# Laying a block diagonal by SBUF-to-SBUF transfers from SyncE, and one mean made earlier

## Chip, cores and metric

One core of a Trainium2 chip runs the kernel. The metric is the device time of one execution in microseconds.

## The reference

The kernel computes a small feed-forward block with a conditioned input. x is 32 x 32 x 256 (batch, channel, feature), 1024 token rows in all.

```python
w = weights[conditions]                       # 32 of 200 matrices, each 32 x 32
xc = jnp.einsum('bct,bcd->bdt', x, w)         # channel mix, per batch item
def _rmsnorm(x, g): return g * (x * rsqrt(mean(x * x) + EPS))
def _act_quant(x):                            # 8-bit steps per row
    scale = 127.0 / clip(max(abs(x)), 0.0001)
    return clip(round(x * scale), -128, 127) / scale
def _ternary_quant(w):
    s = mean(abs(w))
    return round(tanh(w / (s + EPS))) * arctanh(s)
def _linear_bit(x, w, g): return einsum('bsd,od->bso', _act_quant(_rmsnorm(x, g)), _ternary_quant(w))
h = silu(_linear_bit(xc, w1, g1)) * _linear_bit(xc, w2, g2)     # hidden width 1024
out = x + _linear_bit(h, w3, g3)
```

## The kernel before

The 1024 token rows are eight tiles of 128 rows, worked on as four pairs in the first half and tile by tile in the second. Every engine has its own program, written out by hand, and runs it in order; semaphores join them. There is no planner.

The first half prepares the operands. A tile holds four batch items of 32 channels, so the channel mix of a tile is one matmul with a 128 x 128 block diagonal, `cw_diag[:, tile, :]`, of four gathered 32 x 32 matrices. GpSimd zeroes `cw_diag` (L214, `diag_zero`), then gathers the rows of the condition weights by eight indirect transfers, one for a tile (L218), into `cw_rows`; `cw_in[p]` reaches 32 when both tiles of pair p have landed. On VectorE `diagonal(p)` (L441 to L446) copies the 32 x 32 blocks of pair p from `cw_rows` onto the diagonal with four copies, one for each group of 32 partitions and both tiles at once. TensorE's `condition(p)` (L645 to L654) waits for these four copies and for the x of the pair and makes `xc_ps`. ScalarE's `x_squares(p)` (L348) takes the sums of squares, VectorE's `x_gains(p)` (L471) multiplies by g1 and g2, `x_peak_of(p)` takes the largest magnitude, `x_scales(p)` the scale; `x_round(p)` is split between GpSimd and ScalarE (all VectorE for pair 3). TensorE's `x_turn(p)` transposes and VectorE's `x_keep(p)` writes the operand.

Weights: each of W1, W2, W3 is loaded in two halves of 512 KB (L159). The sums of magnitudes are made by ScalarE for first halves and by VectorE for second halves of W1 and W2 (`abs_sum_half`, L434), by ScalarE for both halves of W3. TensorE's `total(m)` adds over partitions, VectorE's `mean(m)` (L448 to L455) gives the mean and its inverse, ScalarE's `tanh(m)` (L344) uses it, `round_w(m)` rounds (W1 on VectorE, W2 and W3 on GpSimd), `w_turn` transposes, `keep_w` writes.

Orders around the change:

- SyncE (L164 to L191): cond; W1 half 0, W1 half 1, W2 half 0; W2 half 1 behind W1 half 0; x pair 0 behind W1 half 1; g1 and g2 behind W2 half 0; x pair 1 behind W2 half 1; W3 half 0 behind x pair 0; W3 half 1 behind x pair 1; x pair 2 behind W3 half 0; x pair 3 behind W3 half 1; g3 behind x pair 2; then the eight stores.
- VectorE (L512 to L540): two half sums, mean(0), diagonal(0), mean(1), diagonal(1), round_w(0), x_gains(0), x_peak_of(0), diagonal(2), x_gains(1), diagonal(3), x_scales(0), x_peak_of(1), mean(2), keep_w(0, 1), x_gains(2), and so on.
- TensorE (L705 to L718): total(0), total(1), condition(0), condition(1), the two w_turn of W1, condition(2), total(2), condition(3), x_turn(0), the two w_turn of W2, x_turn(1).
- ScalarE (L374 to L392): two half sums, tanh(0), x_squares(0), tanh(1), x_squares(1), the two half sums of W3, x_squares(2), x_round(0), keep_w_a(0), tanh(2), x_round(1), x_squares(3), keep_w_a(1), x_round(2), the logarithm.
- GpSimd (L281 to L293): x_roots(0), x_roots(1), round_w(1), x_round(0), x_roots(2), arctanh_start, x_round(1), x_roots(3), x_round(2), arctanh_rest, arctanh_end, round_w(2). arctanh_end releases `xdeq_ready`, for which the first gate (`silu(0)`, L399) waits.

The second half runs over eight tiles: two up projections, gate, product, RMS norm with g3 on GpSimd (L325), rounding, transposes, down projection, residual and store.

Of the kernel before, what the change touches and what calls it, by code (L numbers as in the profile page):

```python
# [14 lines left out]
BATCH, CHAN, FEAT = 32, 32, 256  # L15
HID = 1024
TOKENS = BATCH * CHAN
TILES = TOKENS // P
PAIRS = TILES // 2
PER_TILE = P // CHAN  # L20
# [13 lines left out]
def adaln_ffn(nc, x, cond, cond_w, w1, g1, w2, g2, w3, g3, out):  # L34
    ctx = ExitStack()
    with ctx:
        def sb(name, shape, dt=FP32):
            return ctx.enter_context(nc.sbuf_tensor(name, shape, dt))

        def sem(name):  # L40
            return ctx.enter_context(nc.semaphore(name))
# [22 lines left out]
        cw_rows = sb("cw_rows", [P, TILES, CHAN])  # L64
        cw_diag = sb("cw_diag", [P, TILES, P])
# [55 lines left out]
        cw_in = [sem(f"cw_in{p}") for p in range(PAIRS)]  # L121
# [3 lines left out]
        xr_a, wq_a, neg_made = sem("xr_a"), sem("wq_a"), sem("neg_made")  # L125
        rounder_made, roots_made, diag_zero = sem("rounder_made"), sem("roots_made"), sem("diag_zero")
        cond_cast, chan_made, idx_summed, idx_ready = sem("cond_cast"), sem("chan_made"), sem("idx_summed"), sem("idx_ready")
        diag_ready = [sem(f"diag{p}_ready") for p in range(PAIRS)]

        abs_a, abs_v, tot_ready, mean_ready, inv_ready = sem("abs_a"), sem("abs_v"), sem("tot_ready"), sem("mean_ready"), sem("inv_ready")  # L130
        tanh_done, w_rounded, wt_ready, wq_ready = sem("tanh_done"), [sem(f"w{m + 1}_rounded") for m in range(3)], sem("wt_ready"), sem("wq_ready")
# [23 lines left out]
        @block.sync  # L155
        def _(sp):
            def load_w(m, h):
                n = w_sb[m].shape[1] // 2
                sp.dma_start(w_sb[m][:, h * n:(h + 1) * n, :], w_rows[m][:, h * n:(h + 1) * n, :]).then_inc(w_in[m][h], 16)  # L159

            def load_x(p):
                sp.dma_start(x_sb[:, 2 * p:2 * p + 2, :], x_rows[:, 2 * p:2 * p + 2, :]).then_inc(x_in[p], 16)

            sp.dma_start(cond_i[:], cond.rearrange("(t b) -> b t", b=PER_TILE), allow_slow_non_contiguous=True).then_inc(cond_in, 16)  # L164
            load_w(0, 0)
            load_w(0, 1)
            load_w(1, 0)

            sp.wait_ge(w_in[0][0], 16)
            load_w(1, 1)  # L170
            sp.wait_ge(w_in[0][1], 16)
            load_x(0)
            sp.wait_ge(w_in[1][0], 16)
            for k, g in enumerate((g1, g2)):
                sp.dma_start(g12[:, k, :], g.partition_broadcast(P)).then_inc(g12_in, 16)
            sp.wait_ge(w_in[1][1], 16)
            load_x(1)
            sp.wait_ge(x_in[0], 16)
            load_w(2, 0)
            sp.wait_ge(x_in[1], 16)  # L180
            load_w(2, 1)
            sp.wait_ge(w_in[2][0], 16)
            load_x(2)
            sp.wait_ge(w_in[2][1], 16)
            load_x(3)
            sp.wait_ge(x_in[2], 16)
            sp.dma_start(g3_all[:], g3.partition_broadcast(P)).then_inc(g3_in, 16)
            for t in range(TILES):
                sp.wait_ge(out_ready, t + 1)
                sp.dma_start(out_rows[:, t, :], x_sb[:, t, :]).then_inc(stored, 16)  # L190
            sp.wait_ge(stored, 16 * TILES)  # L191
# [233 lines left out]
        def _(dve):  # L425
# [8 lines left out]
            def abs_sum_half(m):  # L434

                n = w_sb[m].shape[1] // 2
                dve.wait_ge(w_in[m][1], 16)
                dve.tensor_reduce(abs_sum[:, 2 * m + 1:2 * m + 2], w_sb[m][:, n:, :], AX.XY, ALU.add,  # L438
                                  apply_absolute_value=True).then_inc(abs_v, 1)

            def diagonal(p):  # L441

                dve.wait_ge(cw_in[p], 32)
                for b in range(PER_TILE):
                    s = slice(b * CHAN, (b + 1) * CHAN)
                    dve.tensor_copy(cw_diag[s, 2 * p:2 * p + 2, s], cw_rows[s, 2 * p:2 * p + 2, :]).then_inc(diag_ready[p], 1)  # L446

            def mean(m):  # L448

                dve.wait_ge(tot_ready, m + 1)  # L450
                dve.tensor_scalar(mean_abs[:, m:m + 1], tot_ps[m], 1.0 / n_weights, None, ALU.mult).then_inc(mean_ready, 1)
                dve.wait_ge(mean_ready, m + 1)
                dve.tensor_scalar(eps_mean[:, m:m + 1], mean_abs[:, m:m + 1], EPS, None, ALU.add).then_inc(mean_step, 1)
                dve.wait_ge(mean_step, m + 1)
                dve.reciprocal(inv_mean[:, m:m + 1], eps_mean[:, m:m + 1]).then_inc(inv_ready, 1)  # L455

            def round_w(m):
                dve.wait_ge(tanh_done, m + 1)
                dve.tensor_scalar(w_sb[m][:], w_sb[m][:], ROUNDER, None, ALU.add).then_inc(w_rounded[m], 1)
# [11 lines left out]
            def x_gains(p):  # L471

                dve.wait_ge(xss_ready, 2 * (p + 1))
                if p == 0:
                    dve.wait_ge(g12_in, 32)
                for k in range(2):
                    dve.tensor_tensor(xg[:, p, k], xc_ps[p % 2],  # L477
                                      g12[:, k, :].unsqueeze(1).to_broadcast([P, 2, FEAT]), ALU.mult).then_inc(xg_ready, 1)

            def x_peak_of(p):  # L480
                dve.wait_ge(xg_ready, 2 * (p + 1))
                dve.tensor_reduce(x_peak[:, p], xg[:, p], AX.X, ALU.max,  # L482
                                  apply_absolute_value=True).then_inc(xpeak_ready, 1)

            def x_scales(p):

                dve.wait_ge(xpeak_ready, p + 1)
                dve.wait_ge(xroot_ready, p + 1)
                dve.scalar_tensor_tensor(x_step[:, p], x_peak[:, p], 1.0 / QMAX,
                                         x_root[:, p, 0, :].unsqueeze(1).to_broadcast([P, 2, 2]), ALU.mult, ALU.max  # L490
                                         ).then_inc(xstep_ready, 1)
                dve.wait_ge(xstep_ready, p + 1)
                dve.reciprocal(x_scale[:, p], x_step[:, p]).then_inc(xscale_ready, 1)
                dve.tensor_tensor(x_deq0[:, p], x_step[:, p],
                                  x_root[:, p, 1, :].unsqueeze(1).to_broadcast([P, 2, 2]), ALU.mult).then_inc(xdeq0_ready, 1)
# [14 lines left out]
                                  ALU.add).then_inc(xq_ready, 1)  # L510

            abs_sum_half(0)  # L512
            abs_sum_half(1)
            mean(0)
            dve.wait_ge(diag_zero, 1)
            diagonal(0)
            mean(1)
            diagonal(1)
            round_w(0)
            x_gains(0)  # L520
            x_peak_of(0)
            diagonal(2)
            x_gains(1)
            diagonal(3)
            x_scales(0)
            x_peak_of(1)
            mean(2)
# [113 lines left out]
        def _(pe):  # L641
# [2 lines left out]
            pe.matmul(idx_ps, group32[:], cond_f[:], start=True, stop=True).then_inc(idx_summed, 1)  # L644
            def condition(p):  # L645

                pe.wait_ge(diag_ready[p], PER_TILE)
                pe.wait_ge(x_in[p], 16)
                if p >= 2:
                    pe.wait_ge(xg_ready, 2 * (p - 1))  # L650
                for i in range(2):
                    last = pe.matmul(xc_ps[p % 2][:, i, :], cw_diag[:, 2 * p + i, :], x_sb[:, 2 * p + i, :],  # L652
                                     start=True, stop=True)
                last.then_inc(xc_ready, 1)  # L654
# [51 lines left out]
            total(0)  # L706
            total(1)
            condition(0)
            condition(1)
            w_turn(0, 0)  # L710
            w_turn(0, 1)
            condition(2)
            total(2)
            condition(3)
# [98 lines left out]
```

## Time and profile before

| | us |
|---|---|
| median of 3 runs | 78.03 |
| lowest and highest run | 77.39, 78.25 |
| span of the profiled execution, first to last instruction | 76.6 |
| busy in the span: VectorE, GpSimd, TensorE, ScalarE | 58.1, 55.4, 48.0, 47.7 |

The page has no time of the profiled execution beside its span, so the span is set beside the runs. VectorE is the busiest engine over the whole span, but busy shares are averages over two halves with different limits. The first half ends where the first gate starts, at 34.47 us. "Idle before" in a timeline is the time in which the engine did nothing, with what ended it.

### The profile page before, as it was taken

The page shows a single profiled execution, that of the slowest core. Times are in us where ns is not written, and L with a number is a line of the kernel's source. Part 1 is how long each engine was busy: PE and PEld are TensorE (multiplying, and loading weights), DVE is VectorE, ACT ScalarE, POOL GpSimd, SP SyncE. Part 2 cuts the span into 40 slices and gives each one's busy share as a digit, 9 for nine tenths or more (in the row PEclk, how much of TensorE's full clock was granted, in tenths as well). Part 3 has the DMA queues.
Part 4 walks back from the last instruction along what each step waited for, and adds up shares of the span by engine and source line. Part 5 has one row for each costly group of instructions (what it writes and reads, how often), then busy time and mean ns, then how long its engine had stood idle before and what let it go on. Part 6 is the DMA issues. An engine that isn't in the chain of part 4 may idle for free.

```text
span 76.6 us, 1068 instructions
## 1 busy us (share of the span) xinstructions
PE 48.0 (63%) x298; PEld 31.3 (41%) x302; DVE 58.1 (76%) x117; ACT 47.7 (62%) x70; POOL 55.4 (72%) x97
## 2 busy tenths in 40 slices
PE   0200509995829803999897298977888471079960
PEld 0200408774526702355461155544545250078730
DVE  0203278989999999967699989979797979996340
ACT  5014508599909995995859959896979783410000
POOL 6788777264938977989689898999999999810100
PEclk9999999999975895556999999999999999855589
DMA  0599989963710000000000000010202020010222
GB/s 0 119 385 346 327 237 278 330 210 115 253 71 0 0 0 4 0 9 4 0 0 0 0 0 4 17 52 9 68 0 68 0 68 0 23 45 0 68 68 68
DMA packets 5369, 6.22 MB, mean 81 GB/s; under 512 B 500, under 2 KB 4980, under 8 KB 5364
## 3 DMA queue, kind: packets, MB, share of 16 engines
q1 hardware_dynamic: 5108, 6.03, 24.6%
q0 software_dynamic: 256, 0.13, 0.8%
q8 instruction: 2, 0.03, 0.2%
q14 instruction: 3, 0.02, 0.1%
HBM read 5.11 MB, written 1.05 MB: 80 GB/s over the span
## 4 chain that ended last, share of the span: by engine, by line
DVE 24%; issue 22%; POOL 22%; DMA 12%; PE 11%; ACT 4%; SPq 0%; POOLq 0%; DVEq 0%
DMA w_sb<-in_L_ffn_w 12%; POOL hg L325 11%; PE y_ps L769 6%; DVE xg L477 6%; DVE cw_diag L446 5%; DVE x_peak L482 5%; PE a_ps L652 3%; PE t_ps L758 2%; POOL h_deq L302 2%; DVE hid L551 2%; ACT hr L413 2%; DVE abs_sum L438 2%; POOL h_root L316 2%; POOL h_base L311 2%; POOL h_base L309 1%
## 5 line engine op out<-in xcount | busy, mean ns | idle before, releaser
L325 POOL TENSOR_TENSOR hg<-hid,g_all 128x1024 f32<-128x1024 f32 x7 | 16.5, 2358 | 0.8 <-DVE hid L551 0.8
L413 ACT ACTIVATE hr<-hg,rounder,h_scale 128x1024 f32<-128x1024 f32 x7 | 8.7, 1241 | 5.5 <-DVE h_scale L574 5.5
L769 PE MATMUL y_ps<-w_t,hq_t 128*128 128x256 bf16 x64 | 10.3, 319 | 2.1 <-DVE hq_t L581 2.0
L560 DVE TENSOR_REDUCE h_peak<-hg 128x1 f32<-128x1024 f32 x8 | 9.7, 1217 | 1.7 <-POOL hg L325 1.6
L551 DVE SCALAR_TENSOR_TENSOR hid<-v_ps,x_deq,gate 128x1024 f32<-128x1024 f32 x8 | 10.2, 1271 | 0.9 <-PE v_ps L725 0.6
L725 PE MATMUL v_ps<-w_t,xq_t 128*128 128x512 bf16 x30 | 8.9, 415 | 3.0 <-DVE hid L551 2.9
L399 ACT ACTIVATE gate<-a_ps,x_deq 128x1024 f32<-128x1024 f32 x8 | 8.8, 1100 | 2.2 <-PE a_ps L725 2.1
L725 PE MATMUL a_ps<-w_t,xq_t 128*128 128x512 bf16 x30 | 8.7, 407 | 1.8 <-issue 1.3
L218 POOL DMA_INDIRECT cw_rows<-in_L_cond_weights,row_idx x8 | 7.9, 982 | 2.4 <-issue 2.1
L769 PEld LDWEIGHTS y_ps<-w_t,hq_t 128*128 128x128 bf16 x64 | 6.9, 115 | 5.6 <-DVE hq_t L581 4.1
L652 PE MATMUL a_ps<-x_sb,cw_diag 128*128 128x256 f32 x16 | 7.0, 597 | 2.5 <-DVE cw_diag L446 2.5
L758 PE MATMUL t_ps<-ident,hr 128*128 128x128 f16 x64 | 5.8, 243 | 4.2 <-ACT hr L413 4.2
L406 ACT ACTIVATE h_sq_junk<-hid 128x1024 bf16<-128x1024 f32 x8 | 8.4, 1046 | 0.0
L341 ACT ACTIVATE abs_values<-w_sb 128x1024 bf16<-128x1024 f32 x4 | 4.2, 1061 | 5.2 <-DMA w_sb<-in_L_ffn_w 5.2
L346 ACT ACTIVATE w_sb<-w_sb,inv_mean 128x2048 f32<-128x2048 f32 x3 | 6.0, 1999 | 2.2 <-DVE inv_mean L455 2.2
L667 PE MATMUL y_ps<-abs_sum,ones 128*128 128x1 f32 x12 | 2.5, 317 | 7.6 <-DVE abs_sum L438 7.2
L758 PEld LDWEIGHTS t_ps<-ident,hr 128*128 128x128 f16 x64 | 4.8, 110 | 6.0 <-ACT hr L413 4.7
L438 DVE TENSOR_REDUCE abs_sum<-w_sb 128x1 f32<-128x1024 f32 x2 | 2.4, 1220 | 5.4 <-DMA w_sb<-in_L_ffn_w 5.4
L302 POOL TENSOR_SCALAR h_deq<-h_step,h_root,atanh 128x1 f32<-128x1 f32 x8 | 3.6, 455 | 3.5 <-DVE x_sb L588 3.5
L316 POOL TENSOR_TENSOR h_root<-h_base,roots 128x2 f32<-128x2 f32 x8 | 5.6, 702 | 0.7
L725 PEld LDWEIGHTS v_ps<-w_t,xq_t 128*128 128x128 bf16 x32 | 2.8, 104 | 7.8 <-DVE hid L551 5.0
L581 DVE TENSOR_SCALAR hq_t<-t_ps 128x1024 bf16<-128x1024 f16 x8 | 5.5, 683 | 0.6 <-PE t_ps L758 0.6
(76 smaller groups left out, 99.9 us busy)
## 6 DMA issues: line engine op xcount, KB each, us to landing
w_sb<-in_L_ffn_w SPq DMA_DIRECT2D x6, 512.0 KB, 4.5
x_sb<-in_x SPq DMA_DIRECT2D x4, 256.0 KB, 3.1
out<-x_sb SPq DMA_DIRECT2D x8, 128.0 KB, 1.7
g_all<-in_L_ffn_g SPq DMA_DIRECT2D x1, 512.0 KB, 4.3
g<-in_L_ffn_g SPq DMA_DIRECT2D x2, 128.0 KB
cw_rows<-in_L_cond_weights,row_idx POOLq DMA_INDIRECT x8, 4.3
cond_i<-in_itok_B SPq DMA_DIRECT2D x1, 0.1 KB
```

What stands on the lines that cost most here:

```text
L218: pool.indirect_dma_start(cw_rows[:, t, :], None, cond_rows, bass.IndirectOffsetOnAxis(ap=row_idx[:, t:t + 1].bitcast(UINT32), axis=0)).th ...
L316: pool.tensor_tensor(h_root[:, b], h_base[:, b], roots[:, :, 0], ALU.pow).then_inc(hroot_ready, 1)
L325: pool.tensor_tensor(hg[:, b], hid[:, b], g3_all[:], ALU.mult).then_inc(hg_ready, 1)
L399: act.activation(gate[:, t % 2], a_ps[:], ACT.Silu, scale=x_deq[:, 0, t // 2, t % 2:t % 2 + 1]).then_inc(gate_ready, 1)
L406: act.activation(h_sq_junk[:, t % 2], hid[:, t % 2], ACT.Square, accum_out=h_ss[:, t % 2:t % 2 + 1]).then_inc(hss_ready, 1)
L413: act.activation(hr[:, t % 2], hg[:, t % 2], ACT.Identity, scale=h_scale[:, t % 2:t % 2 + 1], bias=rounder[:]).then_inc(hr_ready, 1)
L551: dve.scalar_tensor_tensor(hid[:, t % 2], v_ps[:], x_deq[:, 1, t // 2, t % 2:t % 2 + 1], gate[:, t % 2], ALU.mult, ALU.mult).then_inc(hid_ ...
L560: dve.tensor_reduce(h_peak[:, b], hg[:, t % 2], AX.X, ALU.max, apply_absolute_value=True).then_inc(hpeak_ready, 1)
L652: last = pe.matmul(xc_ps[p % 2][:, i, :], cw_diag[:, 2 * p + i, :], x_sb[:, 2 * p + i, :], start=True, stop=True)
L725: last = pe.matmul(ps[:, n * HALF:(n + 1) * HALF], xq_t[:, which, c, t * P:(t + 1) * P], w_t[which][:, c, n * HALF:(n + 1) * HALF], start= ...
L758: last = pe.transpose(t_ps[t % 2][:, j * P:(j + 1) * P], low_half(hr[:, t % 2, j * P:(j + 1) * P]), ident[:])
L769: last = pe.matmul(y_ps[t % 2][:, 0:FEAT], hq_t[:, t % 2, j, :], w_t[2][:, j, :], start=(j == 0), stop=(j == KH - 1))
```

## The change

- The copies of `diagonal` leave VectorE. SyncE gets a `diagonal(i)` of its own, with i = 0, 1, 2 for pair 0, pair 1, and pairs 2 and 3 together. It waits for the gathers of these pairs and issues four transfers from `cw_rows` to `cw_diag`, one for each group of 32 partitions: 32 partitions by two tiles (four tiles for i = 2) by 128 bytes.
- They are placed in SyncE's order: diagonal(0) behind x pair 0 (with a wait for the zeroed tile), diagonal(1) behind x pair 1, diagonal(2) behind x pair 2.
- TensorE's `condition(p)` waits for the transfers (64 counts of `diag_in`) instead of the four copies; pairs 2 and 3 share one semaphore.
- VectorE's `mean(0)` moves ahead of `abs_sum_half(1)`, the sum of W2's second half.

```diff
-        diag_ready = [sem(f"diag{p}_ready") for p in range(PAIRS)]
+        diag_in = [sem(f"diag_in{i}") for i in range(3)]
@@ SyncE
+            def diagonal(i):
+
+                for p in ((0,), (1,), (2, 3))[i]:
+                    sp.wait_ge(cw_in[p], 32)
+                tiles = slice(2 * i, (2, 4, TILES)[i])
+                for b in range(PER_TILE):
+                    s = slice(b * CHAN, (b + 1) * CHAN)
+                    sp.dma_start(cw_diag[s, tiles, s], cw_rows[s, tiles, :]).then_inc(diag_in[i], 16)
+
@@
             load_w(1, 1)
             sp.wait_ge(w_in[0][1], 16)
             load_x(0)
+            sp.wait_ge(diag_zero, 1)
+            diagonal(0)
             sp.wait_ge(w_in[1][0], 16)
             for k, g in enumerate((g1, g2)):
                 sp.dma_start(g12[:, k, :], g.partition_broadcast(P)).then_inc(g12_in, 16)
             sp.wait_ge(w_in[1][1], 16)
             load_x(1)
+            diagonal(1)
             sp.wait_ge(x_in[0], 16)
             load_w(2, 0)
             sp.wait_ge(x_in[1], 16)
             load_w(2, 1)
             sp.wait_ge(w_in[2][0], 16)
             load_x(2)
+            diagonal(2)
             sp.wait_ge(w_in[2][1], 16)
             load_x(3)
@@ VectorE
-            def diagonal(p):
-
-                dve.wait_ge(cw_in[p], 32)
-                for b in range(PER_TILE):
-                    s = slice(b * CHAN, (b + 1) * CHAN)
-                    dve.tensor_copy(cw_diag[s, 2 * p:2 * p + 2, s], cw_rows[s, 2 * p:2 * p + 2, :]).then_inc(diag_ready[p], 1)
-
@@
             abs_sum_half(0)
+            mean(0)
             abs_sum_half(1)
-            mean(0)
-            dve.wait_ge(diag_zero, 1)
-            diagonal(0)
             mean(1)
-            diagonal(1)
             round_w(0)
             x_gains(0)
             x_peak_of(0)
-            diagonal(2)
             x_gains(1)
-            diagonal(3)
             x_scales(0)
@@ TensorE, condition(p)
-                pe.wait_ge(diag_ready[p], PER_TILE)
+                pe.wait_ge(diag_in[min(p, 2)], 16 * PER_TILE)
```

## Rows read from the trace of the kernel before

**Rows 1.** Stretches: us, busy of each engine (instructions), granted clock, DMA share, GB/s

```profile
34.50:64.00 29.50, 23.13 (x167) 12.76 (x168) 26.23 (x40) 24.00 (x30) 26.91 (x34) 0.98 0.06 19
```

**Rows 2.** Chain of waits from 8 to 35 us: start, us, what

```profile
12.65 2.09 PE a_ps L652 x4
14.76 0.85 ACT x_sq_junk L351 x4
...
20.24 1.59 DVE cw_diag L446
...
30.54 0.94 POOL xr L243 x2
...
34.47 1.12 ACT gate L399
```

**Rows 3.** Timeline of SyncE's queue: start, us, line, what, idle before

```profile
6.91 0.37 SPq L162 DMA_DIRECT2D x_sb<-in_x  x1
8.46 0.83 SPq L175 DMA_DIRECT2D g<-in_L_ffn_g  x2
10.10 0.38 SPq L162 DMA_DIRECT2D x_sb<-in_x  x1
10.91 2.35 SPq L159 DMA_DIRECT2D w_sb<-in_L_ffn_w  x2
15.05 2.64 SPq L162 DMA_DIRECT2D x_sb<-in_x  x2
```

**Rows 4.** The page's list of issues: KB each, median us from issue to landing

```profile
out<-x_sb SPq DMA_DIRECT2D x8, 128.0 KB, 1.7
```

**Rows 5.** Line L218, all eight gathers: ns min/median/max, first and last start, landing

```profile
L218 POOL DMA_INDIRECT cw_rows<-in_L_cond_weights,row_idx x8: 944/944/1237, 3.8 to 12.9; - x8
...
DMA to landing us min/median/max: 3.6/4.3/4.9
```

**Rows 6.** Line L218 in the window of gather 1 alone

```profile
L218 POOL DMA_INDIRECT cw_rows<-in_L_cond_weights,row_idx x1: 955/955/955, 5.4 to 5.4; - x1
...
DMA to landing us min/median/max: 4.9/4.9/4.9
```

**Rows 7.** Timeline of TensorE, 8 to 20 us

```profile
8.28 0.98 PE L667 MATMUL y_ps<-abs_sum,ones 128*128 128x1 f32 x4 [5.03 <-DVE abs_sum L438]
...
16.22 1.91 PE L702 MATMUL t_ps<-ident,w_sb 128*128 128x128 f16 x16
18.97 1.13 PE L652 MATMUL a_ps<-x_sb,cw_diag 128*128 128x256 f32 x4 [0.84 <-DVE cw_diag L446]
```

**Rows 8.** Timeline of VectorE, 10 to 29 us

```profile
10.10 1.22 DVE L438 TENSOR_REDUCE abs_sum<-w_sb 128x1 f32<-128x1024 f32 x1 [1.97 <-DMA w_sb<-in_L_ffn_w]
...
20.15 2.33 DVE L446 COPY cw_diag<-cw_rows 32x64 f32<-32x64 f32 x4
...
23.98 0.15 DVE L451 TENSOR_SCALAR mean_abs<-y_ps 128x1 f32<-128x1 f32 x1
...
28.87 1.28 DVE L477 TENSOR_TENSOR xg<-a_ps,g 128x512 f32<-128x512 f32 x2
```

**Rows 9.** The tile of the gathered rows: the copies

```profile
L446 DVE COPY cw_diag<-cw_rows x16: 163/186/1671, 11.7 to 22.3; 32x64 f32<-32x64 f32 x16
```

**Rows 10.** Line L159, the six loads of the weights

```profile
DMA to landing us min/median/max: 4.1/4.5/6.2
```

**Rows 11.** Line L162, the four loads of x

```profile
DMA to landing us min/median/max: 2.7/3.1/4.0
```

**Rows 12.** Timeline of ScalarE, 20 to 28 us

```profile
20.17 0.39 ACT L351 ACTIVATE x_sq_junk<-a_ps 128x256 bf16<-128x256 f32 x1
...
22.92 1.09 ACT L358 ACTIVATE xr<-xg,rounder,x_scale 128x256 f32<-128x256 f32 x2 [1.90 <-DVE x_scale L493]
...
27.79 0.36 ACT L351 ACTIVATE x_sq_junk<-a_ps 128x256 bf16<-128x256 f32 x1
```

**Rows 13.** Timeline of GpSimd at 20 us

```profile
19.88 1.91 POOL L237 TENSOR_SCALAR w_sb<-w_sb 128x2048 f32<-128x2048 f32 x1
```

## Prediction

> **What bounds the kernel now.** I read the table of stretches first. From 34.5 to 64.0 us GpSimd is busy 26.91 of 29.50 us [rows 1]: a steady loop over the eight token tiles, in which nothing that the change touches is issued. So the change can only shift the moment at which that loop starts, and I take any shift of it one for one to the end. The span is 76.6 us; the runs around it are 78.03 us in the median, so 1.4 us lie outside the span, and I leave those as they are.
>
> The chain of waits says what sets that start [rows 2]. It enters the first matmul of `condition(0)` at 12.65, goes over ScalarE's squares and then stays almost wholly on VectorE until 30.5, where GpSimd's last `x_round` and the arctanh steps lead to the first gate at 34.47. The copies of `diagonal` lie on that chain: sixteen, in the median 186 ns [rows 9], so a group of four takes about 0.9 us with its gaps, but the group of `diagonal(3)` takes 2.33 us [rows 8], since its first copy, the longest of all (1671 ns), covers 1.59 us of the chain [rows 2, 9]. Read alone, this says that VectorE would win some 3 us in the stretch behind 18 us. ScalarE's timeline says how much room there is beside it: it idles only 1.90 us ahead of `x_round(0)` at 22.92, and then works without a gap to the squares of pair 3 at 27.79 [rows 12], whose end (28.6) comes 0.26 us ahead of `x_gains(3)` at 28.87 [rows 8]. So the second limit is 0.26 us away, and it begins with what releases ScalarE at about 21 us: the squares of pair 2, hence `condition(2)` on TensorE, which starts at 18.97 [rows 7].
>
> SyncE's own timeline is the view that decides [rows 3]. It is one in-order queue, and before the change its waits only touch transfers of their own kind. It shows each load's issue; the landings are in the answers on the lines [rows 4, 5, 10, 11].
>
> **The change part by part.**
>
> *1. mean(0) moved ahead of the sum of W2's half.* VectorE idles 1.97 us before that sum at 10.10 [rows 8]. The total of W1 can be made at once behind the first half sum: its four short matmuls run from 8.28 to 9.26 [rows 7], so mean(0) runs at 9.3 to 9.9, inside that idle time, and the tanh of W1 starts near 9.9 instead of 11.8. Its price is nothing (if the cover were gone, it would cost its own 0.5 us). Its gain is nothing either: what follows the tanh on ScalarE is the squares of pair 0, which wait for TensorE at 14.76 [rows 2], and mean(1) still waits for the half sum that starts at 10.10.
>
> *2. Sixteen copies leave VectorE.* That frees two groups of 0.9 us ahead of `round_w(0)`, which comes forward by about 1 us into nothing that waits (TensorE turns W1 behind condition(1)), and 0.9 + 2.33 us around x_gains(1). After it, `x_scales(0)` can follow `x_gains(1)` at 20.2. VectorE's next fixed point is mean(2), now at 23.98 [rows 8], which needs total(2), and total(2) stands behind `condition(2)` in TensorE's order. So this gain counts only as far as `condition(2)` allows.
>
> *3. Twelve transfers enter SyncE's queue, each group behind a wait for the gathers.* What an SBUF-to-SBUF transfer costs is not shown before. Issue: the nearest rows are the 256 KB loads of x (0.37 to 0.38 us each) and the two gains (0.83 us for two) [rows 3]; I take 0.36 us, so 1.44 us for four, with bounds of 0.33 and 0.5. Landing: the stores of 128 KB need 1.7 us and x's 256 KB need 2.7 at least [rows 4, 11]; a diagonal transfer carries 8 to 16 KB, in runs of 128 bytes. The line through these two rows falls by 1 us for 128 KB, so it reaches 0.7 us at no bytes: the lower bound. The upper one is x's median of 3.1 [rows 11], for a transfer that is held up by the loads ahead of it. I take the nearest row, 1.7.
>
> Now the queue, instruction by instruction. Gather 1, the second of pair 0, starts at 5.4 and lands 4.9 us later, at 10.3 [rows 6]. SyncE, free since 7.3, stands there: g1 and g2, before at 8.46, and load_x(1), before at 10.10, are queued behind that wait. diagonal(0) issues from 10.3 to 11.75; g1 and g2 to 12.6 (they land well before 15.6, when x_gains(0) wants them); load_x(1) at 12.6, 2.5 us late, landing 2.8 to 3.1 later at 15.4. diagonal(1) has its gathers and issues from 13.0 to 14.45. load_w(2,0) goes out at 14.45 instead of 10.91, load_w(2,1) at 15.4 behind load_x(1), instead of 12.9. The first lands after 4.1 to 4.5 us [rows 10], say at 18.7, and that releases load_x(2) at 18.7 instead of 15.05 [rows 3]. diagonal(2), which now holds pairs 2 and 3, has its last gather by then (last start 12.9, 4.9 us at most) [rows 5] and issues from 19.1 to 20.55; its last transfer starts at 20.2 and lands at 21.9. x's pair 2 lands 2.7 to 3.1 us behind 18.7, at 21.4 to 21.8. So `condition(2)` starts at 21.9 instead of 18.97 [rows 7]: 2.9 us late. load_x(3) goes out at 20.55 and lands by 23.7, before TensorE is through total(2); g3 lands near 26 and is wanted in the second half.
>
> The earlier pairs: condition(0) has its diagonal at 11.4 + 1.7 = 13.1 instead of 12.65, condition(1) at 15.7; the squares of pair 1 end near 18.7, and the two halves of W3, landed at 18.7 and 19.7, are summed on ScalarE by 20.9. None of it is late for 21.9.
>
> *4. What follows from it.* condition(2) takes 1.2 us until the squares start (18.97 to 20.17) [rows 7, 12], where its neighbour condition(0) takes 2.1 [rows 2]: the same matmuls at an upper and a lower rate. condition(1) from 15.7 and the turn of W1's halves (1.91 us) end near 19.7, so at 21.9 TensorE will have idled about 2 us, against 0.84 before [rows 7]: either rate may hold. The squares take 0.85 [rows 2]. `x_round(0)` then starts at 21.9 + 1.2 + 0.85 = 23.95, or at 24.85, against 22.92: 1.0 or 1.9 us late. ScalarE has no gap from there to the squares of pair 3, so they end 1.0 or 1.9 late, less the 0.26 of slack: x_gains(3), x_scales(2), GpSimd's x_round(2) at 30.54 and the gate at 34.47 come 0.75 or 1.65 us late. VectorE's own chain asks for less: total(2) takes 0.98 us at the lower rate [rows 7] behind condition(2), so mean(2) comes at 24.1 to 25.0 against 23.98 [rows 8]. I take the middle, 1.2 us, since the rows leave both rates open: 78.03 + 1.2 = 79.2 us.
>
> A rule and a row: the fourth copy group was stretched by a GpSimd operation. GpSimd's round_w(1) runs 19.88 to 21.79 and the copy that covers 1.59 us of the chain from 20.24 ends with it [rows 2, 13]. If x_scales(0), which comes to stand there, inherits the stall until about 22.1, x_peak_of(1) ends at 23.7 and VectorE is only 0.3 us ahead of its 23.98, even with condition(2) early. The Trainium skill, page SBUF — State Buffer, section Who interferes with whom, says that VectorE and GpSimd lock one port pair for a whole instruction, also where the VectorE operation has two SBUF inputs and GpSimd's reads SBUF, as x_scales and round_w(1) would. By that rule the trace agrees for a copy; no row of before shows it for x_scales. The skill's page DMA: Bandwidth & Descriptors (section Anatomy of one DMA) gives about 2.0 us of fixed cost per transfer; by it the sum would be 0.3 us more, 79.5 as an estimate from that page.
>
> **The rivals.**
>
> *Opposite side: VectorE's freed time reaches the end.* If condition(2) started before about 20.1, ScalarE would round pair 0 at 20.1 + 1.2 + 0.85 = 22.15, 0.8 early, and VectorE, 3 us lighter, would follow. With condition(2) at 19.5 ScalarE is 1.1 us early (it cannot do more: the halves of W3 are summed until about 20.9) and the kernel stands at 76.9. For it speaks that the chain of waits names the copies; against it, that 1.8 us would have to be saved in a queue whose steps are a landing of a gather, eight issues, a 4.1 us landing and another 1.7, and that VectorE may meet round_w(1) again. Chance 0.13.
>
> *The loads' delay is swallowed.* If the issues cost 0.33 (eight of them stand before load_x(2), 0.24 us less) and the transfers land in 0.7, x's pair 2 is the later input, at 18.45 + 2.7 = 21.1. Then x_round(0) starts at 21.1 + 1.2 + 0.85 = 23.15 at the upper rate, 0.23 late, which the slack of 0.26 swallows: no change, 78.0; with one of the three only in part, up to 78.8. Chance 0.30.
>
> *Small transfers are dear.* At 0.5 us per issue, twelve of them put 12 × 0.14 = 1.7 us more before condition(2), and a landing of 3.1 us adds 1.4: 79.2 + 1.7 to 3.1, so 80.9 to 82.3. Against it: the issues of x and of the gains cost 0.37 to 0.42 [rows 3], with more bytes and more runs. Chance 0.12.
>
> *Forecast:* condition(2) is 2.5 to 3.5 us late, +0.8 to +2.2, so 78.8 to 80.3. Chance 0.45.
>
> **The numbers.** About 1% (0.78 us) is what a measurement of this kernel can tell from no change. Faster by more: the first rival, 0.13. Within it: 0.30. Slower: 0.45 + 0.12 = 0.57. The range takes in the forecast, most of the swallowed case and the start of the dear one: 77.8 to 80.9.
>
> **What the profile after would show.** The first diagonal issue at about 10.3, 0.36 us apart, landing 1.7 later; load_x(1) at 12.6; load_w(2,0) at 14.5; load_x(2) at 18.7; condition(2) at 21.9 with a wait for a DMA in front of it; ScalarE idle before the squares of pair 2 and not behind them; the first gate at 35.2 to 36.1; the loop from there unchanged in length. I am wrong if condition(2) starts before 21, if ScalarE has gaps between 24 and 29 us, or if another input than pair 2's diagonal ends the wait.

## The result, and the profile after

| | before | after |
|---|---|---|
| median of the runs, us (4 each) | 77.90 | 82.26 |
| span of the profiled execution | 76.6 | 80.8 |
| first gate starts | 34.47 | 38.60 |
| from the first gate to the end of the span | 42.1 | 42.2 |

The changed kernel takes 1.056 times the time of the kernel before, 95% interval 1.050 to 1.062: 4.4 us slower. Here and below the ratios are of fast runs, those within 1.5% of the fastest of their kernel. Slower was forecast, but 79.2 us with an upper end of 80.9 was too little. The whole loss stands in front of the first gate, which comes 4.13 us late; from there on the two executions last the same, so the one-for-one rule of the prediction held.

The chain of waits of the changed kernel (start, us, what) has left VectorE. It runs along SyncE's queue:

```profile
5.37 4.93 DMA cw_rows<-in_L_cond_weights,row_idx
...
10.38 0.71 SPq L168
...
11.13 0.59 SPq L168
...
17.19 3.87 DMA w_sb<-in_L_ffn_w
...
21.07 0.38 SPq L171
...
23.48 1.82 DMA cw_diag<-cw_rows
...
25.34 1.20 PE a_ps L653 x4
```

Gather 1 lands at 10.30, as forecast. Each diagonal transfer then holds the queue 0.6 us, not 0.36. The last of the third group starts at 23.48, lands 1.82 us later, and condition(2) starts at 25.34, where [rows 7] had it at 18.97.

SyncE's own timeline answers to [rows 3]:

```profile
10.38 2.63 SPq L168 DMA_DIRECT2D cw_diag<-cw_rows  x4
13.05 1.06 SPq L186 DMA_DIRECT2D g<-in_L_ffn_g  x2
14.15 0.43 SPq L171 DMA_DIRECT2D x_sb<-in_x  x1
14.63 2.51 SPq L168 DMA_DIRECT2D cw_diag<-cw_rows  x4
17.19 1.06 SPq L159 DMA_DIRECT2D w_sb<-in_L_ffn_w  x2
21.07 0.38 SPq L171 DMA_DIRECT2D x_sb<-in_x  x1
21.55 2.53 SPq L168 DMA_DIRECT2D cw_diag<-cw_rows  x4
```

From 10.38 to 18.25 the queue issues without a pause. g1 and g2 take 1.06 us where [rows 3] had 0.83. load_w(2,0) goes at 17.19 instead of 10.91, and load_x(2) at 21.07 instead of 15.05.

The tile of the block diagonal, all twelve transfers (ns min/median/max of an issue, then us to landing):

```profile
L168 SPq DMA_DIRECT2D cw_diag<-cw_rows x12: 587/597/712, 10.4 to 23.5; - x12
...
DMA to landing us min/median/max: 1.8/1.9/2.9
```

ScalarE shows how the delay is carried on, as in [rows 12]:

```profile
26.56 0.38 ACT L364 ACTIVATE x_sq_junk<-a_ps 128x256 bf16<-128x256 f32 x1 [2.98 <-PE a_ps L653]
...
27.29 1.08 ACT L371 ACTIVATE xr<-xg,rounder,x_scale 128x256 f32<-128x256 f32 x2
...
32.14 0.37 ACT L364 ACTIVATE x_sq_junk<-a_ps 128x256 bf16<-128x256 f32 x1
```

It idles 2.98 us in front of the squares of pair 2, and then nothing stands idle to the squares of pair 3, 4.85 us after x_round(0) began (4.87 before). x_round(0) is 4.37 us late; less the 0.26 us of slack that makes 4.11, and the gate is 4.13 late.

### The profile page after: what moved, and what is told of

It is laid out like the page before. It is cut to its first block, busy times and chain, and to the rows that moved or that the text cites. A ratio compares the mean times of both kernels' runs of the same rounds, so it can differ in the third digit from the quotient of the medians.

```text
span 80.8 us, 1069 instructions
## 1 busy us (share of the span) xinstructions
PE 49.0 (61%) x302; PEld 32.0 (40%) x302; DVE 53.6 (66%) x101; ACT 47.8 (59%) x70; POOL 55.8 (69%) x97
## 4 chain that ended last, share of the span: by engine, by line
POOL 28%; issue 21%; DMA 13%; PE 12%; SPq 11%; ACT 10%; DVE 1%; POOLq 0%; DVEq 0%
POOL hg L338 10%; SPq L168 8%; DMA cw_rows<-in_L_cond_weights,row_idx 6%; PE y_ps L770 6%; DMA w_sb<-in_L_ffn_w 5%; ACT xr L371 3%; PE t_ps L759 2%; DMA cw_diag<-cw_rows 2%; PE a_ps L726 2%; POOL h_deq L315 2%; POOL h_root L329 2%; ACT x_sq_junk L364 2%; ACT hr L426 2%; POOL cw_rows L231 2%; PE a_ps L653 1%
## 5 line engine op out<-in xcount | busy, mean ns | idle before, releaser
L770 PE MATMUL y_ps<-w_t,hq_t 128*128 128x256 bf16 x64 | 10.3, 318 | 1.6 <-DVE hq_t L582 1.6
L483 DVE TENSOR_TENSOR xg<-a_ps,g 128x512 f32<-128x512 f32 x8 | 5.1, 684 | 5.2 <-ACT x_sq_junk L364 5.2
L364 ACT ACTIVATE x_sq_junk<-a_ps 128x256 bf16<-128x256 f32 x8 | 3.0, 378 | 9.0 <-PE a_ps L653 9.0
L653 PEld LDWEIGHTS a_ps<-x_sb,cw_diag 128*128 128x128 f32 x16 | 4.2, 291 | 8.8 <-DMA cw_diag<-cw_rows 8.1
L238 POOL TENSOR_SCALAR x_base<-x_ss 128x2 f32<-128x2 f32 x4 | 0.8, 192 | 8.3 <-ACT x_sq_junk L364 8.3
```

The source lines that it names most:

```text
L770: last = pe.matmul(y_ps[t % 2][:, 0:FEAT], hq_t[:, t % 2, j, :], w_t[2][:, j, :], start=(j == 0), stop=(j == KH - 1))
```

## The experiments

One number is needed to read them. The last sixteen matmuls of the down projection took 3.15 us in the profiled execution of before, 3.12 after, and anything from 2.00 to 3.12 in the others, and from the first gate to the end the others took 40.6 to 42.1 us. So the profiled executions differ by about 1 us in a stretch that no change touches, and I compare the start of the first gate in the traces and the ratio in the repeated runs. The code shows only the lines that carry an experiment; declarations, and waits that go with them, are not shown.

### What an issue costs (e1_probe)

```diff
+            for b in range(4):                               # (a); five more groups like it
+                s = slice(b * CHAN, (b + 1) * CHAN)
+                sp.dma_start(cw_spare[s, 0:2, s], cw_rows[s, 0:2, :]).then_inc(probed, 16)
+            sp.wait_ge(probed, 64)
```

> The kernel before, with 24 spare transfers issued by SyncE in its idle time between g3's landing (about 23 us) and the first store (about 49 us), to tiles that nothing reads; six groups of four, each behind the landing of the group before: (a) the diagonal form, 32 partitions x 2 x 128 bytes SBUF to SBUF; (b) the same destination from x in HBM; (c) 32 partitions, 256 contiguous bytes, SBUF to SBUF; (d) 128 partitions, 256 contiguous bytes, SBUF to SBUF; (e) 128 partitions x 2 x 128 bytes, SBUF to SBUF; (f) 128 partitions x 1 KB from HBM. Theory 1 (the 0.6 us that an issue took in the changed kernel belongs to SBUF as the source): a, c, d, e at 0.6, b and f at 0.33 to 0.4. Theory 2 (it belongs to transfers of 32 partitions): a, b, c at 0.6, d, e, f below 0.4. Theory 3 (it comes from the traffic at 10 to 24 us, loads and gathers in flight): all below 0.4 here. The whole time within 1% of before under each.

The probe's SyncE timeline, groups a to f in order:

```profile
22.57 2.68 SPq L196 DMA_DIRECT2D cw_spare<-cw_rows  x4
26.45 1.75 SPq L200 DMA_DIRECT2D cw_spare<-in_x  x4
29.40 2.47 SPq L204 DMA_DIRECT2D probe_flat<-cw_rows  x4
33.06 2.45 SPq L207 DMA_DIRECT2D probe_flat<-cw_rows  x4
36.78 3.73 SPq L210 DMA_DIRECT2D cw_spare<-cw_rows  x4
41.83 1.78 SPq L213 DMA_DIRECT2D probe_flat<-in_x  x4
```

Theory 1 holds for these six forms. With nothing else in flight, the four groups that copy from SBUF to SBUF take 0.59 to 0.63 us for an issue (median), whether they cover 32 partitions or 128, in runs of 128 or 256 bytes. The two that read HBM take 0.43, a little above the expected 0.40: (b) with the very same destination as (a), and (f) with 128 KB. One issue of (e) took 1.71 us; that stays unexplained. The landings are much alike for (a) and (b), 1.8 and 1.6 us in the median; (f) needed 2.1 and (e) 2.7. The probe was run once and took 78.25 us beside 77.68.

All six groups write SBUF, so the probe varies the source alone. The eight stores of the kernel before read SBUF too, and write HBM. Their line (ns min/median/max of an issue) shows that an SBUF source alone is not dear:

```profile
L190 SPq DMA_DIRECT2D out<-x_sb x8: 332/332/360, 48.8 to 74.5; - x8
```

What costs 0.6 us is thus the transfer with both ends in SBUF. The stores also differ from the probe's groups in their spacing (one at a time) and in their size, 128 KB, and no run varies the destination alone.

### Does the lateness of the loads cost it, or that of the diagonal? (e2_copies_stay)

```diff
+                    sp.dma_start(cw_spare[s, tiles, s], cw_rows[s, tiles, :]).then_inc(spare_in[i], 16)
             # same waits, same places as the change; VectorE's copies and TensorE's waits as before
```

> VectorE's copies and mean(0) as before; SyncE waits for the gathers and issues the same twelve transfers at the same places, but to a spare tile that nothing reads. Theory (the delay of the loads behind the issues costs the time): load_x(2) still issues near 21.1 and lands near 24.3, condition(2) waits for x and starts near 24.3 instead of 25.3: about 81.2 us, ratio to before 1.035 to 1.05. Rival (the late landing of the diagonal itself costs it): no more than 1% over before.

Ratio 1.052, interval 1.040 to 1.064 (81.30 beside 77.68). load_x(2) issued at 20.71, condition(2) started at 23.39 and the first gate at 37.62. The transfers write a tile that nobody reads, and most of the loss is there: 3.15 of the 4.13 us at the gate, and in the runs 1.052 against 1.056. TensorE's timeline has condition(2) and condition(3):

```profile
23.39 1.30 PE L668 MATMUL a_ps<-x_sb,cw_diag 128*128 128x256 f32 x4 [2.17 <-issue]
...
27.00 2.05 PE L668 MATMUL a_ps<-x_sb,cw_diag 128*128 128x256 f32 x4 [1.67 <-issue]
```

It is not the same path all the way, though. Of the 3.15 us only 2.3 come through condition(2) and ScalarE (x_round(0) at 25.46, 2.54 late, less 0.26). The rest comes through load_x(3), which issues at 23.78 behind the third group: condition(3) waits for it until 27.00, the turn of W2 behind it ends late, and x_gains(3) begins at 32.02, 0.9 us behind the squares that it follows at once in the changed kernel. There the late diagonal holds condition(2) until 25.34, 1.95 us later than here, and the gate comes 0.98 later.

### Waits alone, issues alone (e6_waits_only, e9_issues_only)

```diff
 e6          load_x(0)
+            sp.wait_ge(cw_in[0], 32)         # likewise cw_in[1], and cw_in[2], cw_in[3]
 e9          load_x(0)
+            sp.wait_ge(rows_made, 1)
+            diagonal(0)                      # from spare_rows to cw_spare, no wait for gathers
```

> The kernel before with SyncE's waits for the gathers at the places of the change, and no transfer. Theory (the waits alone hold little: g1 goes at 10.3, load_x(1) at 11.2, load_x(2) at 16 instead of 15.05, x's pair 2 lands at 19.3 against condition(2) at 18.97): 77.9 to 78.3 us, ratio 1.000 to 1.006. Rival (the head of the queue standing at the gathers is a main part of the loss): ratio above 1.015.

> The kernel before with twelve transfers of the same form at the same places of SyncE's queue, from a spare tile that is ready at 4 us to another spare tile, with no wait for the gathers; VectorE's copies stay. Theory (the issues, 0.6 us each, are the loss, the waits are not): diagonal(0)'s four issue from 7.3 to 9.9, g1 and g2 at 9.9, load_x(1) at 11, load_w(2,0) near 14, load_x(2) near 18.5, x's pair 2 lands near 21.8; condition(2) near 21.8: 78.6 to 79.6 us, ratio 1.015 to 1.03, less than with the waits (1.052), since the first four issues now fall into time in which SyncE stood idle. Rival (waits and issues each cost nothing alone): ratio below 1.007.

Waits alone: ratio 0.998 (0.993 to 1.003), first gate at 34.80. Issues alone: 1.011 (1.007 to 1.016), gate at 34.94. The second fell short of what I expected (1.015 to 1.03): load_x(2) went at 17.89, half a microsecond earlier, and its x landed for a condition(2) at 20.64 and not 21.8. The two do not add up to the 1.052 of both together. SyncE's timeline of the run with issues only shows one reason:

```profile
7.20 2.62 SPq L170 DMA_DIRECT2D cw_spare<-spare_rows  x4
9.86 1.06 SPq L188 DMA_DIRECT2D g<-in_L_ffn_g  x2
10.96 0.44 SPq L173 DMA_DIRECT2D x_sb<-in_x  x1
11.45 2.51 SPq L170 DMA_DIRECT2D cw_spare<-spare_rows  x4
14.00 1.06 SPq L163 DMA_DIRECT2D w_sb<-in_L_ffn_w  x2
17.89 0.38 SPq L173 DMA_DIRECT2D x_sb<-in_x  x1
```

The first four issues run from 7.20 to 9.82, time in which SyncE had stood idle but for the gains. With the wait in front of them the same four begin at 10.38, and everything behind starts 3.2 us later (load_x(1) at 14.15 against 10.96). An issue is nearly free while it falls into idle time, and the wait takes that idle time away. load_w(2,0), at 10.91 before, goes at 11.73 with the waits alone, at 14.00 with the issues alone and at 16.90 with both (e2): 0.8, 3.1 and 6.0 us late, so 2.1 us more together than the sum.

The other reason lies behind the queue. The waits alone are not free in the queue: load_x(2) went at 17.05, not at the expected 16, and condition(2) started as late as with the issues alone (TensorE's timelines of e6 and e9):

```profile
20.65 2.04 PE L656 MATMUL a_ps<-x_sb,cw_diag 128*128 128x256 f32 x4 [1.01 <-issue]
```

```profile
20.64 2.05 PE L670 MATMUL a_ps<-x_sb,cw_diag 128*128 128x256 f32 x4 [2.79 <-issue]
```

In both, condition(2) is 1.7 us late and runs at TensorE's lower rate besides (2.0 us instead of 1.13). What swallows that is ScalarE's idle 1.90 us ahead of x_round(0) [rows 12], where it waits for VectorE anyway: x_round(0) starts at 23.45 and 23.46, half a microsecond late. With both parts condition(2) is 4.42 us late, which that idle time no longer covers. The two gates, 34.80 and 34.94, are nearly the same, so the traces do not show what sets the ratios 0.998 and 1.011 apart.

### The count and the price of the issues (e5_half, e12_hbm_source)

```diff
 e5
-                for b in range(PER_TILE):
+                for b in range(0, PER_TILE, 2):
 e12
-                    sp.dma_start(cw_spare[s, tiles, s], cw_rows[s, tiles, :]).then_inc(spare_in[i], 16)
+                    sp.dma_start(cw_spare[s, tiles, s], x_rows[s, tiles, 0:CHAN]).then_inc(spare_in[i], 16)
```

> The changed kernel with two of the four transfers of each group (groups of partitions 0 and 2 only; half of the diagonal blocks stay zero, so the output is not that of the reference). A group then holds SyncE for 2 x 0.64 = 1.3 us, which is about what four were taken to cost in the prediction (1.44). Theory (the prediction's queue was right and only the price of an issue was off): load_x(2) issues at 18.5, condition(2) starts at 21.6 to 21.9, ScalarE's x_round(0) about 1 us late, 78.7 to 79.6 us, ratio to before 1.012 to 1.025. Rival (the wait for the gathers and the landings carry the loss whatever the number of issues): ratio above 1.035.

> As the run in which the copies stay (waits for the gathers, twelve transfers of 32 partitions x 2 or 4 x 128 bytes to a spare tile, VectorE's copies as before), but the transfers read x in HBM instead of the gathered rows in SBUF. In the probe four such issues took 1.75 us instead of 2.68. Theory (the price of an issue with an SBUF source is what the prediction had wrong): a group holds SyncE for 1.75 us, load_x(2) issues near 19.2 instead of 20.7, condition(2) starts near 22.3, ratio 1.02 to 1.035 against 1.052. Rival (only bytes and landings matter, not the issue): ratio 1.045 or above.

With half the issues: ratio 1.031 (1.021 to 1.041), 79.61 us. load_x(2) went at 18.88, 0.4 us behind the expectation, and x_round(0) started at 24.89. The first gate at 36.20 is 1.73 us late. That this is close to the upper of the two values of the prediction (1.65) is chance: that value stood for a condition(2) at 21.9 and the lower rate, and here it ran at the upper one. condition(2), at 22.99, was a microsecond later than expected, since here the last transfers landed slowly, with two loads still in flight:

```profile
L168 SPq DMA_DIRECT2D cw_diag<-cw_rows x2: 597/600/602, 19.4 to 20.0; - x2
...
DMA to landing us min/median/max: 2.5/2.7/3.0
```

The measured ratio lies between theory and rival; its interval reaches into the expected range, and the four runs scatter from 78.59 to 80.30. It is well below 1.056, so the number of transfers counts, but part of what is left is landings.

With the HBM source, the count kept and the copies staying: 1.017 (1.001 to 1.034) against 1.052 (1.040 to 1.064) for the same kernel with the SBUF source. The twelve issues took 428 ns in the median instead of 597:

```profile
L170 SPq DMA_DIRECT2D cw_spare<-in_x x12: 328/428/465, 10.9 to 21.7; - x12
```

The intervals don't touch, which speaks for the price of an issue as a cause. But the 1.017 rests on the two shorter of four runs (77.98 and 79.05; the others took 79.28 and 80.19); the medians of all, 79.16 beside 77.43, give 1.022. Each of the four is below each of those with the SBUF source (80.93 and more).

The profiled execution was the longest of the four, and its timeline bears out only the queue's part. From the first of these issues to load_x(2) it took 8.94 us (10.92 to 19.86) where the SBUF source took 10.61 (10.10 to 20.71). But the first issue, which waits for gather 1, came 0.8 us later there, pair 2's x took 3.3 us to land instead of 2.6, and condition(2) ran at TensorE's lower rate. So condition(2) started at 23.28 and not at the expected 22.3 (23.39 with the SBUF source), and the gates are 37.42 and 37.62. That the shorter issues reach the end is shown by the run times alone.

### What VectorE's freed time is worth (e3_no_diagonal, e4_pair3)

```diff
 e3: no copies, no transfers; condition(p) waits for diag_zero alone
 e4          load_x(3)
+            sp.wait_ge(cw_in[3], 32)
+            for b in range(PER_TILE):
+                s = slice(b * CHAN, (b + 1) * CHAN)
+                sp.dma_start(cw_diag[s, 6:8, s], cw_rows[s, 6:8, :]).then_inc(diag3_in, 16)
 e4 (VectorE)
-            diagonal(3)
```

> The kernel before without any work for the block diagonal: neither copies nor transfers, the matmuls of the channel mix run on the zeroed tile, so the output is not that of the reference. It shows how much the freed time of VectorE can be worth at most. Theory (VectorE's copies lie on the chain but ScalarE is close behind): the first gate 1.5 to 2 us earlier, 76.2 us, ratio 0.975 to 0.985. Rival (ScalarE's 0.26 us of slack is all there is): ratio 0.995 or above.

> The kernel before, with one part of the change alone: only pair 3's blocks go by transfer, four of them issued by SyncE behind load_x(3), where no load but g3 stands behind them; the copies of pairs 0 to 2 stay. Issues from 17.8, at 0.64 us each, to 20.3, landing at 21.7 to 22.1; condition(3) starts near 22 as before at 22.5; VectorE loses the 2.33 us group ahead of x_scales(0). Theory (the transfers hurt only by what stands behind them in the queue): faster than before, 76.4 us, ratio 0.975 to 0.985, x_scales(0) at 20.3. Rival (x_scales(0) meets GpSimd's round_w(1) and is stretched to 21.8 as the copy was): ratio 0.99 to 1.0.

Without any diagonal work: ratio 0.976 (0.965 to 0.986), 75.70 us, gate at 33.27. So VectorE's copies are worth 1.2 us at the gate, once nothing is paid for them.

With only pair 3 by transfer: 0.989 (0.978 to 1.001), 76.45 beside 77.68 in the medians, gate at 33.31, as early as without any copies. The interval just reaches 1, so the gain rests on the gate, and on e10 below. That is the one placement in the queue where four issues at 0.6 us have nothing behind them but g3: they ran from 16.87 to 19.49. The gain is 1.16 us at the gate and not the 1.6 that lay behind the expected 76.4 us (78.03 less 76.4). VectorE's timeline of this kernel shows what took the rest, and GpSimd's what it stood beside:

```profile
18.66 1.29 DVE L483 TENSOR_TENSOR xg<-a_ps,g 128x512 f32<-128x512 f32 x2
19.87 1.65 DVE L495 SCALAR_TENSOR_TENSOR x_step<-x_peak,x_root 128x4 f32<-128x4 f32 x1
21.55 0.18 DVE L499 RECIPROCAL x_scale<-x_step 128x4 f32<-128x4 f32 x1
```

```profile
19.59 1.92 POOL L243 TENSOR_SCALAR w_sb<-w_sb 128x2048 f32<-128x2048 f32 x1
21.83 0.94 POOL L249 TENSOR_SCALAR xr<-xg,x_scale 128x256 f32<-128x256 f32 x2 [0.32 <-DVE x_scale L499]
```

An operation on 4 elements per partition, 0.15 us elsewhere, takes 1.65 us and ends as round_w(1) does (19.59 + 1.92 = 21.51). It inherited the stall of the copy it replaced.

### Taking the stall away (e8_pair3_swap, e11_swap_only)

```diff
             x_roots(1)
-            round_w(1)
             x_round(0)
+            round_w(1)
```

> Pair 3 by transfer as in the run before, and in GpSimd's order x_round(0) ahead of round_w(1), so that x_scales(0), which took 1.65 us there beside round_w(1), meets no long operation of GpSimd. Theory (the stall is the one port pair that VectorE with two SBUF inputs and GpSimd share): x_step(0) takes 0.16 us at 19.9, ScalarE's x_round(0) starts at 20.8 instead of 21.8, the first gate at 32.3 to 32.5 instead of 33.3: about 75.4 us, ratio 0.965 to 0.98. Rival (the 1.65 us was a wait for x_root or another input): x_step(0) still ends at 21.5, ratio as the run before, 0.984.

> The kernel before with GpSimd's x_round(0) ahead of round_w(1) and nothing else: all copies stay, no transfer. Theory (the 1.67 us copy was a stall behind round_w(1)): the group of diagonal(3) takes 0.83 us, x_scales(0) ends at 21.4 instead of 22.8; but GpSimd's round_w(1), x_roots(2) and the arctanh steps come later, as in the run with both, where the first gate waited for GpSimd at 33.6: gate at 33.6 to 34.0, ratio 0.987 to 0.997. Rival (the stall moves to another VectorE operation beside round_w(1)): ratio 0.998 or above.

In both, the stall is gone. VectorE's timeline with pair 3 by transfer and the swap:

```profile
20.15 0.15 DVE L495 SCALAR_TENSOR_TENSOR x_step<-x_peak,x_root 128x4 f32<-128x4 f32 x1
```

and in the kernel before with the swap alone the copies of diagonal(3) take 0.83 us instead of 2.33:

```profile
19.73 0.83 DVE L446 COPY cw_diag<-cw_rows 32x64 f32<-32x64 f32 x4
```

But neither kernel wins by it. The ratios are 0.987 (0.977 to 0.997), beside 0.989 without the swap, and 1.000 (0.997 to 1.004). ScalarE's timeline of the first says where it went:

```profile
33.64 1.11 ACT L405 ACTIVATE gate<-a_ps,x_deq 128x1024 f32<-128x1024 f32 x1 [1.44 <-POOL x_deq L285]
```

The gate now waits 1.44 us for GpSimd, whose x_roots(2) and arctanh steps stand behind round_w(1), moved back. The expected 75.4 us was wrong: it counted ScalarE's earlier start and forgot that GpSimd's order sets the end of the same stage. With the swap alone the gate is at 33.98 in the trace, after 1.30 us of waiting for GpSimd, as expected, where the runs show no gain: 1.000, the number of the rival, whose reason did not show, since no VectorE operation beside round_w(1) was stretched. Why the 0.5 us at the gate does not reach the runs is open; it is less than the scatter named above.

### mean(0) alone, and the version that beats both (e7_mean_only, e10_pair3_mean)

```diff
             abs_sum_half(0)
+            mean(0)
             abs_sum_half(1)
-            mean(0)
```

> The kernel before with mean(0) ahead of abs_sum_half(1) and nothing else. Theory (it moves a tanh into idle time and nothing that waits for it is on the path): tanh of W1 at 9.9 instead of 11.8, the first gate where it was, ratio 0.997 to 1.003. Rival (VectorE and ScalarE come through their first orders earlier and keep some of it): ratio 0.99 or below.

> The two parts that did not hurt, together: pair 3 by transfer behind load_x(3), copies for pairs 0 to 2, and mean(0) ahead of abs_sum_half(1). Theory: the gain of the one (ratio 0.989) and what the other shows (0.994) come from different stretches, so 0.978 to 0.985, first gate at 33.1 to 33.3, 76.1 us. Rival (mean(0) is worth nothing and its 0.994 is scatter): 0.987 to 0.991. Faster than both the kernel before and the changed one under each.

mean(0) alone: 0.994 (0.989 to 0.999), gate at 34.26 against 34.47, between theory and rival and nearer the theory. What it is worth is at most some tenths of a microsecond; the ten runs hardly tell it from nothing.

Pair 3 by transfer and mean(0) early: 0.986 (0.979 to 0.992), 76.39 us beside 77.43, gate at 33.39. That is faster than the kernel before, where the changed kernel stands at 1.056. The ratio lies between what theory (0.985 at most) and rival (0.987 at least) gave, so it does not tell whether the mean adds anything: the gate is no earlier than with pair 3 alone (33.31).

## Why the prediction was right in direction and wrong in size

*The end moves one for one with the first gate.* Right: 42.1 and 42.2 us behind it, though the other executions show that this stretch varies by over 1 us.

*mean(0) costs nothing and gains nothing.* Right within 0.2 us at the gate (e7).

*The queue is the place.* Right. The order of events was the forecast one: SyncE stands at gather 1 until 10.3, g1, g2 and load_x(1) come behind the four transfers, load_w(2,0) behind the next four, load_x(2) behind its landing, and condition(2) waits for the last transfer of the third group. The rival in which VectorE's time reaches the end did not come; it needed condition(2) before 20.1, and it came at 25.34. One of the signs of being wrong did come, gaps on ScalarE between 24 and 29 us: it idled until 26.56. That is the forecast idle time in front of the squares of pair 2, moved by the late condition(2), and not a gap behind them.

*The price of an issue.* This is the step that failed. I took 0.36 us, with 0.5 as the upper bound, from the rows nearest in size [rows 3]. All of them are loads from HBM. The twelve transfers cost 597 ns in the median, and about 0.04 us between two. Eight of them stand ahead of load_x(2) and three ahead of the start of the last one, so up to condition(2) eleven issues count: 11 × (0.64 - 0.36) = 3.1 us. The gains behind them (1.06 us instead of 0.83), load_x(1) and a slightly later start add 0.4, the gap ahead of the third group and the landing of its last transfer 0.2, and load_w(2,0)'s landing gives 0.4 back (3.87 us against the 4.25 assumed). Together that is 3.3 of the 25.34 - 21.9 = 3.4 us. The bound of 0.5 was no bound, since no row of before has both ends in SBUF. The stores, which read SBUF and write HBM at 0.33 us, would have misled in the same way. e1 shows the price with one destination and two sources, and e5 and e12 show that fewer or cheaper issues give part of the loss back.

*The landing.* 1.7 us was close: 1.82 for the transfer that counted, 1.7 to 1.9 for this form with nothing in flight (e1), up to 2.9 in the changed kernel and 2.5 to 3.0 in e5. The 2.0 us of the Trainium skill (DMA: Bandwidth & Descriptors, Anatomy of one DMA) that the prediction set beside it stand there for transfers issued from GpSimd; these were issued from SyncE.

*From condition(2) to the gate.* Right to 0.1 us: at the upper rate of TensorE, 3.4 us more at condition(2) than forecast turn the 0.75 us of the sum into 4.15, and 4.13 were measured. I had taken the middle of two rates; condition(2) ran at the upper one (1.20 us to the squares), so 0.45 us of the 1.2 forecast were too much, which hid a part of the other error.

*The dear-transfer rival* had half of the right mechanism, with 0.12 of the chance. It put 0.5 us per issue, which gives 80.9, and reached 82.3 only by a landing of 3.1 us. The measured 82.26 lies just within its span, but by issues of 0.64 and a landing of 1.82, so that is partly luck. It also counted twelve issues ahead of condition(2) where eleven stand there.

*The forecast's span.* By the prediction's own two rates a condition(2) that is 2.5 us late gives 0.35 or 1.25 us at the gate and one that is 3.5 late gives 1.35 or 2.25. Its "+0.8 to +2.2" took the middle at one end and the lower rate at the other.

*The stall behind round_w(1).* x_scales(0) did inherit it (e4), as feared. The Trainium skill (SBUF — State Buffer, Who interferes with whom) says that a VectorE instruction with two SBUF inputs contends with a GpSimd instruction that reads SBUF. The trace agrees: x_step took 1.65 us beside GpSimd's round_w(1) and 0.15 us without it (e8). In the changed kernel itself it played no part, because x_scales(0) came at 22.75, ahead of round_w(1) at 23.13.

## What to carry to other kernels

A wait and a string of issues put into an in-order queue must be priced together: each was nearly free here (0.998 and 1.011), and both together cost 5%. The wait took away the idle time in which the issues would have hidden, and the engine behind the queue had 1.90 us of idle time to swallow one delay and not both. Price an issue by a row with the same source and the same destination; where the trace has none, as here, put such transfers into idle time of the queue and measure them first. And where transfers replace copies, put them where nothing urgent stands behind them in the queue: four at the end of the loads brought the gate 1.2 us forward, where twelve in their midst put it 4.1 us back.

## What the runs showed of the hardware that I had not expected

- An issue on SyncE's queue took 0.59 to 0.63 us from SBUF to SBUF and 0.43 from HBM to SBUF, back to back, with nothing else in flight (e1). A store from SBUF to HBM took 0.33, by itself (before); 16 KB and 8 KB transfers cost the same in the changed kernel.
- Loads issued right behind such a string are dearer too: the two gains 1.06 us instead of 0.83, load_x(3) 0.59 instead of 0.38. Behind four issues with an HBM source the gains took 0.90 (e12).
- The last gather took 1.43 us on GpSimd where it had taken 0.94, in the changed kernel, and 1.41 in e5 and 1.60 in e12. In all three VectorE's round_w(0) began within 0.3 us of it, as here in the changed kernel (GpSimd's line, then VectorE's):

```profile
12.87 1.43 POOL L231 DMA_INDIRECT cw_rows<-in_L_cond_weights,row_idx  x1 [0.30 <-issue]
12.89 0.16 DVE L461 RECIPROCAL inv_mean<-eps_mean 128x1 f32<-128x1 f32 x1
12.97 1.21 DVE L465 TENSOR_SCALAR w_sb<-w_sb 128x2048 f32<-128x2048 f32 x1
```

  It cost nothing at the gate of the changed kernel. The Trainium skill (SBUF — State Buffer, SBUF: two separate sides) says that descriptors of GpSimd's DMAs wait while VectorE holds the shared port pair; the trace agrees, with 0.5 us, but no run was made for it alone.
- The last sixteen matmuls of the down projection took 2.00 to 3.15 us in the profiled executions, with the granted clock of the tail at 0.73 of full speed before (64.0 to 76.6 us, matmuls 3.15) and 0.85 in e4 (62.8 to 74.2 us, matmuls 2.00). That alone can move a run by a microsecond.
